# First loads asked for in halves of the partitions by two queues

## What is computed

```python
def _L0_cond_ref(x, language_ids, W, Wr, A, B):
    base = jnp.einsum('btd,od->bto', x, W)
    logits = jnp.einsum('btd,ed->bte', x, Wr)
    bias = jax.nn.one_hot(tgt, E) * LANG_BIAS
    logits = logits + bias[:, None, :]
    topw, topi = jax.lax.top_k(logits, TOP_K)
    weights = jax.nn.softmax(topw, axis=-1)
    gates = jnp.sum(jax.nn.one_hot(topi, E) * weights[..., None], axis=-2)
    h = jnp.einsum('btd,erd->bter', x, A)
    lora_out = jnp.einsum('bter,bte,eor->bto', h, gates, B)
    return base + SCALING * lora_out
x = x + _L0_cond_ref(x, itok_B_0_7, L0_cond_W, L0_cond_Wr, L0_cond_A, L0_cond_B)
```

## Time and profile before

| | |
|---|---|
| time, median of 3 runs | 80.04 us (79.7 to 80.2) |
| time of the profiled execution | 79.61 us |
| its span, first to last instruction | 77.8 us |
| TensorE busy in the span | 74.0 us (95%), 505 products |
| VectorE, ScalarE, GpSimd busy | 48.9, 22.4, 22.6 us |
| HBM read and written | 9.99 and 4.19 MB |

### The profile page before, as it was taken

How to read it: one execution, slowest core, us unless ns; L and a number is a source line. 1 busy time by engine, 2 the same in 40 slices (tenths; PEclk the granted TensorE clock), 3 DMA queues, 4 the chain that set the end, 5 groups by cost and what they waited for, 6 DMA issues and landing times.

```text
span 77.8 us, 1631 instructions
## 1 busy us (share of the span) xinstructions
PE 74.0 (95%) x505; PEld 70.3 (90%) x505; DVE 48.9 (63%) x220; ACT 22.4 (29%) x57; POOL 22.6 (29%) x26
## 2 busy tenths in 40 slices
PE   5979999999999999999999999999999999999960
PEld 2349999899999999999999999999999999999950
DVE  0098958879854829283755739283855739787750
ACT  1647901523503314140504113140404023122100
POOL 4039542055160505123060605123060606000000
PEclk9999999999999999999999999999999999999999
DMA  0999991795597399989900000450000072032143
GB/s 10 308 406 401 419 430 60 167 420 230 83 417 313 54 365 440 383 241 402 388 25 0 0 0 0 177 227 0 0 0 0 0 297 107 0 135 95 44 139 135
DMA packets 3893, 14.24 MB, mean 183 GB/s; under 512 B 432, under 2 KB 1328, under 8 KB 3632
## 3 DMA queue, kind: packets, MB, share of 16 engines
q1 hardware_dynamic: 3600, 13.52, 46.8%
q10 hardware_dynamic: 288, 0.67, 2.2%
HBM read 9.99 MB, written 4.19 MB: 182 GB/s over the span
## 4 chain that ended last, share of the span: by engine, by line
PE 90%; DMA 5%; DVE 1%; ACT 1%; SPq 0%; issue 0%
PE heads_ps L429 43%; PE base_ps L429 28%; PE heads_ps L469 5%; PE base_ps L469 5%; DMA first_sb<-in_first 5%; PE base_ps L473 2%; PE heads_ps L473 2%; PE ghT_ps L460 2%; PE base_ps L453 2%; DVE out_sb L421 1%; ACT w_hi L235 1%; SPq L165 0%; PE warm_ps L460 0%
## 5 line engine op out<-in xcount | busy, mean ns | idle before, releaser
L207 POOL TENSOR_TENSOR x_lo<-xT_sb,x_hi 128x512 fp32r<-128x512 f32 x14 | 18.1, 1294 | 39.0 <-ACT x_hi L242 37.2
L429 PE MATMUL heads_ps<-w_hi,x_hi 128*128 128x392 f32 x64 | 22.2, 357 | 0.0
L429 PE MATMUL heads_ps<-w_hi,x_lo 128*128 128x392 f32 x64 | 21.1, 342 | 0.0
L429 PE MATMUL heads_ps<-w_lo,x_hi 128*128 128x392 f32 x64 | 21.1, 340 | 0.0
L429 PE MATMUL base_ps<-w_hi,x_hi 128*128 128x256 f32 x60 | 16.5, 285 | 0.4 <-ACT w_hi L235 0.4
L429 PE MATMUL base_ps<-w_hi,x_lo 128*128 128x256 f32 x60 | 16.7, 281 | 0.0
L429 PE MATMUL base_ps<-w_lo,x_hi 128*128 128x256 f32 x60 | 16.3, 281 | 0.0
L294 DVE TENSOR_TENSOR ghT_lo<-ghT_ps,ghT_hi 128x128 fp32r<-128x128 f32 x15 | 4.3, 290 | 14.9 <-ACT ghT_hi L246 14.8
L246 ACT ACTIVATE ghT_hi<-ghT_ps 128x128 fp32r<-128x128 f32 x15 | 4.1, 275 | 29.5 <-PE ghT_ps L460 29.5
L429 PEld LDWEIGHTS heads_ps<-w_hi,x_hi 128*128 128x128 f32 x64 | 11.7, 188 | 0.9 <-ACT x_hi L232 0.5
L429 PEld LDWEIGHTS base_ps<-w_hi,x_hi 128*128 128x128 f32 x60 | 11.2, 188 | 0.8 <-ACT w_hi L235 0.8
(11 more groups left out here) (51 smaller groups left out, 98.1 us busy)
## 6 DMA issues: line engine op xcount, KB each, us to landing
x_sb<-in_x SPq DMA_DIRECT2D x4, 768.0 KB, 5.6
out<-out_sb SPq DMA_DIRECT2D x4, 768.0 KB, 4.4
xT_sb<-in_xT SPq DMA_DIRECT2D x3, 768.0 KB, 4.3
xT_sb<-in_xT SPq DMA_DIRECT2D x1, 1024.0 KB, 6.3
x_sb<-in_x SPq DMA_DIRECT2D x1, 1024.0 KB, 9.8
first_sb<-in_first SPq DMA_DIRECT2D x2, 454.0 KB, 5.3
out<-out_sb SPq DMA_DIRECT2D x2, 256.0 KB, 2.0
out<-out_sb SPq DMA_DIRECT2D x4, 128.0 KB, 1.7
```

What stands on the lines that cost most here:

```text
L207: nc.gpsimd.tensor_tensor(x_lo[:, s, :], xT_sb[:, t - len(FIRST), :], x_hi[:, s, :].bitcast(FP32), ALU.subtract).then_inc(x_lo_made, 1)
L429: return nc.tensor.matmul(dst, xs[:, s, chunks[k]], ws[:, k, cols], start=(k == 0 and n == 0), stop=(k == KC - 1 and n == last_n))
```

## The change

The loads of `first` are split in another way. `load_half` asks for one half of the partitions (64 rows) in five transfers: x, ids and head weights of chunk 0 together (652 columns, 2608 bytes of a row), base weights of chunk 0, and chunks 1, 2 and 3 whole. SP calls it for partitions 0 to 63 and ACT for 64 to 127. The semaphores `x_landed` and `wh_landed` become one, `first_landed`; `wb_landed` is now `second_landed`. Each is raised by 16 by each half, so all waits are for 32. SP asks for the third tile's x and all that follows behind its five. The warm-up products are 8, not 9. No other instruction changes.

```diff
-WARM_UP = 9
+WARM_UP = 8
...
+        ahead_of = FIRST_X + IDS + HEADS
+
+        def load_half(engine, rows):
+            engine.dma_start(first_sb[rows, 0, 0:ahead_of], first[rows, 0, 0:ahead_of]).then_inc(first_landed, 16)
+            engine.dma_start(first_sb[rows, 0, ahead_of:], first[rows, 0, ahead_of:]).then_inc(second_landed, 16)
+            for k in range(1, KC):
+                engine.dma_start(first_sb[rows, k, :], first[rows, k, :]).then_inc(chunk_landed[k - 1], 16)
...
-            sp.dma_start(first_sb[:, 0, 0:FIRST_X + IDS], first[:, 0, 0:FIRST_X + IDS]).then_inc(x_landed, 16)
-            sp.dma_start(w_sb[:, 0, base_cols], w[:, 0, base_cols]).then_inc(wb_landed, 16)
-            for k in range(2, KC):
-                sp.dma_start(first_sb[:, k, :], first[:, k, :]).then_inc(chunk_landed[k - 1], 16)
+            load_half(sp, slice(0, P // 2))
             load_xT(2, 1, xT_third)
             sp.dma_start(b_sb[:, :], b).then_inc(b_landed, 16)
...
-            act.dma_start(w_sb[:, 0, heads_cols], w[:, 0, heads_cols]).then_inc(wh_landed, 16)
-            act.dma_start(first_sb[:, 1, :], first[:, 1, :]).then_inc(chunk_landed[0], 16)
-            act.wait_ge(x_landed, 16)
+            load_half(act, slice(P // 2, P))
+            act.wait_ge(first_landed, 32)
             chunk_upper(0)
-            act.wait_ge(wb_landed, 16)
+            act.wait_ge(second_landed, 32)
             w_upper(0, base_cols)
             for k in range(1, KC):
-                act.wait_ge(chunk_landed[k - 1], 16)
+                act.wait_ge(chunk_landed[k - 1], 32)
                 chunk_upper(k)
...
-            dve.wait_ge(wh_landed, 16)
+            dve.wait_ge(first_landed, 32)
             heads_upper(0)
...
-            dve.wait_ge(x_landed, 16)
+            dve.wait_ge(first_landed, 32)
...
-            dve.wait_ge(chunk_landed[0], 16)
+            dve.wait_ge(chunk_landed[0], 32)
```

More of the change, by code:

```diff
@@ L94, in cond_resid_program @@
         warm_ps = ps("warm_ps")
-        x_landed = sem("x_landed")
+        first_landed = sem("first_landed")
         xT_third = sem("xT_third")
@@ L102, in cond_resid_program @@
         x_last = sem("x_last")
-        wh_landed = sem("wh_landed")
-        wb_landed = sem("wb_landed")
+        second_landed = sem("second_landed")
         chunk_landed = [sem(f"chunk_landed{k}") for k in range(1, KC)]
@@ L149, in cond_resid_program @@
         w_sb = first_sb[:, :, FIRST_X + IDS:]
-        w = first[:, :, FIRST_X + IDS:]
+        ahead_of = FIRST_X + IDS + HEADS
[4 more added lines that the diff above has]
+                engine.dma_start(first_sb[rows, k, :], first[rows, k, :]).then_inc(chunk_landed[k - 1], 16)
         block = ctx.enter_context(nc.Block())
```

## The result

| | before | after |
|---|---|---|
| median (lowest to highest), 6 runs each | 79.89 us (79.7 to 80.2) | 82.44 us (82.15 to 82.58) |
| profiled execution | 79.61 us | 82.44 us |
| its span | 77.8 us | 80.6 us |

The ratio is 1.0315, with a 95% interval from 1.0287 to 1.0343. The prediction was 79.9 us, no change, with 0.12 for slower by over 1%. The time lies above the range, which ended at 80.7.

A forecast was written before the change was run, and what follows sets the result against it. TensorE's unbroken run from 5.30 us, released by chunk 0's base weights, was taken to bound the kernel. A 0.05 us gain from the 80.04 median gave 79.99, put at 79.9 us for possibly cheaper issues; range 79.2 to 80.7.

The forecast's parts named there:

- What bounds the kernel now: TensorE's unbroken run of products from 5.30 us, which had waited for chunk 0's base weights, landed at 4.81 us.
- The clock product: First product with a lower part of x, after which all runs without a gap; expected at 5.50 instead of 5.64 us.
- The landing of base weights: Chunk 0's base weights on the DMA queues: at 410 GB/s they land at about 4.1 instead of 4.81 us.
- cover of 0.7 and 0.97 us: Time by which chunk 1's copied weights and chunk 2's were ready before TensorE used them; expected to hold.
- Rival B: DMA transfers: the two halves move slower than 410 GB/s; 80.8 us at 270 GB/s, 82.3 at 205; chance 0.08.
- Its signs: VectorE's first cast later than 4.0 us, or ScalarE waiting on chunks 1 and 2 beyond 6.0 and 7.2.
- The five issues on ACT: ACT's queue: 0.43 us an issue, so the table load ends at 4.20 and `chunk_upper(0)` starts at 4.22, not 3.57.
- The formula: For an issue of i us on ACT, the clock product starts at 3.35 + 5i; the gain is 2.29 - 5i.
- The warm-up: TensorE's start: removing product 9 costs nothing, and the longer pause of some 0.8 us was priced at nothing.
- Rival D: TensorE's pause loses the fast clock, or the step comes late: 1.5 us more, 81.5 us; chance 0.05.
- C, a hidden tail of the table load: On ACT, the table load holds the queue longer than its row: 0.47 us slower, 80.5 us; chance 0.12.
- The sum over rivals: Chances of slower causes: B 0.08, C 0.12, D 0.05; slower by over 1% got 0.12 (B, D, worst of C).

The follow-up runs named there:

- ACT's queue alone: The kernel before with three more small issues of 64 rows on ACT, and 11 warm-up products: 80.33 us (1.0075).
- the transfers alone: The changed kernel with ScalarE's table load ahead of its issues and 12 warm-up products: 82.54 us (1.0318).

## Why the prediction was wrong

- **What bounds the kernel now: right.** The run from 5.30 us is unbroken, and everything lost at the start reached the end. The clock product was the right one to follow: with ACT's queue alone (11 warm-up products) it moved by 0.53 and the time by 0.6. Where loads stay late behind it, it isn't all: with the transfers alone it moved by 1.7 and the time by 2.8.
- **The landing of base weights: wrong, and it is the step that failed.** "As bytes and rate are the same" was taken from transfers of 128 partitions; no row of 64 stood behind it. The rate was 262 GB/s and not 410, the weights came at 6.25 and not at 4.1, and the same assumption stood under chunks 1 to 3, which were given their cover of 0.7 and 0.97 us and no cost. "Same bytes at the same rate" was said of them in so many words. Wrong with it was the reading that, the engines being shared, only the order of the bytes would change: the halves moved fewer bytes in the same time with the engines just as busy.
- **Rival B had the mechanism, with too small a chance (0.08) and too small a price.** For 262 GB/s its own way of counting gives 0.9 us. It priced chunk 2 alone. Chunk 3 is later still (copied at 11.58 with transfers alone, at 7.75 before), and chunk 0 was priced by nothing though, with transfers alone, it was 0.9 us late at the first load and 1.7 at the base weights. Measured alone: 2.8 us. "Both queues are asked at the same moments" was my ground against it, and it was no ground. Its signs all came: VectorE's first cast at 4.30, ScalarE waiting for chunks 1 and 2 until 7.46 and 9.09.
- **The five issues on ACT: mechanism right, size wrong.** I took 0.43 us and called 0.465 the far end above, as if fewer rows could only be cheaper. Measured 0.56 to 0.62, one of 0.86, 3.4 us in all. `chunk_upper(0)` started at 5.48, not 4.22. The formula itself held: with its 5.48 the product would stand at 6.76, just where it stood with 16 warm-up products.
- **The warm-up: the removed product costs nothing, as said; the pause does.** "I price the longer one at nothing" failed. The pause of 0.42 us ahead of 5.30 came after the step to 2.4 GHz and so proved nothing of a pause before it. Rival D's price of 1.5 us was right in size (1.5 to 1.9 in the run with three small issues, if the clock is its cause). In the changed kernel it cost 0.4 at most, as the transfers covered it.
- **C, a hidden tail of the table load: excluded.** The copy began 0.01 us after the load's end, here and in the run with the three issues. The drain that the Trainium skill gives ("ScalarE: Activation LUTs", What ACT_TABLE_LOAD costs) doesn't show behind the first table load of this program.
- **The sum over rivals.** B, C and D were treated as cases of which one happens. Three things happened at once, which together cost no more than the largest of them. The chances don't add up either: B and D alone have 0.13, and slower by over 1% was given 0.12 with the worst of C in it.
- **The sign that was to show me wrong didn't.** "I am wrong above all if ACT's queue isn't what releases `chunk_upper(0)`": it did release it, at 5.48, and the prediction was wrong all the same. The sign watched one of two late things.

## What to carry to other kernels

A price taken from transfers of 128 partitions says nothing of transfers of 64: ask what a changed shape does to the rate and to the issue before counting bytes. The order in which loads land changes with what the other queue asks for at the same moment, so a load that is merged or moved must be followed to the landing of all the others. Where several loads and a queue are late together, the chain of waits names only the last of them; give each its own run, with the others taken away. And see that the remedy of one run (here 16 warm-up products) doesn't become the limit of the next.

## What the runs showed of the hardware

- 64 rows into partitions 0 to 63 moved at 201 to 228 GB/s, 64 rows into 32 to 95 at 335, halves 0 to 63 and 64 to 127 at once at 259 to 272, whole transfers of 128 rows at 376 to 391, halves of the columns on two queues at 390.
- An issue of 64 rows takes 0.60 us at the median, one of 16, 32, 48, 96 or 128 rows 0.42 to 0.45, with 32 bytes a row as with 3632 (measured for 64 and 128 rows). Single issues differ (0.86 and 0.67). The cause is open.
- The step to 2.4 GHz came at 3.65 us in one execution and at about 5.6 in another of almost the same kernel; with TensorE busy from 0.78 us without a pause, at 4.3 and, in another run, not before 6.3. Where TensorE paused before the step, for 0.5 us in one profile and 1.6 in another, it stayed slow until about 9.9 and 9.1. A pause of 1.2 us after the step did nothing; behind one of 3.4 us the granted clock fell to 0.50.
- Chunk 1 on ACT landed at 5.4 when it was asked for 0.46 us ahead of chunk 2 on SP, at 7.2 when both were asked for at the same time, and at 9.4 as the third of its queue, asked for 0.02 us after chunk 2. How the engines choose between two queues isn't explained by any of these runs.
